# Adding x to the mixed terms on VectorE and GpSimd in the fourth layer, with its batches unrolled

## The reference

```
dx = shifted(x) - x
lerpx = x + dx * xw
lora(z, a, b, l) = l + tanh(z @ a.T) @ b.T
r = (x + dx * lora(lerpx, r_la, r_lb, r_ll)) @ rW.T      # and so k, v, g
w = exp(-exp(lora(x + dx * lora(lerpx, d_la, d_lb, d_ll), d_la, d_lb, d_ll)))
kv = k_i * v_j;  y_j = sum_i r_i * (st_ij + u_i * kv_ij);  st = w_i * st + kv     # per head of 8, per token
o = silu(g) * layernorm(y)
x = x + o @ oW.T + ternary_feed_forward(x)
```

## Time and profile before

| | |
|---|---|
| median of 3 runs | 2103.46 us (2102.39 to 2110.44) |
| the profiled execution: own time, span | 2104.47 us, 2102.6 us |
| TensorE busy, share of the span | 1796.5 us, 85% |
| VectorE | 1135.1 us, 54% |
| ScalarE | 925.1 us, 44% |
| GpSimd | 273.4 us, 13% |
| mean granted clock of TensorE | 0.927 |

### The profile page before, as it was taken

The page is one execution under the profiler, slowest core; times in us unless marked ns, Lnnn a source line. Parts: engine busy times, 40 slices in busy tenths (PEclk is TensorE's granted clock), DMA queues, the critical chain, the costliest instruction groups (busy, mean ns, idle before and its releaser), DMA issues. The chain is left out here.

```text
span 2102.6 us, 23302 instructions
## 1 busy us (share of the span) xinstructions
PE 1796.5 (85%) x7982; PEld 1032.2 (49%) x7982; DVE 1135.1 (54%) x1905; ACT 925.1 (44%) x1080; POOL 273.4 (13%) x159
## 2 busy tenths in 40 slices
PE   6699999983289996989899898989898996999996
PEld 3222222222144444666758585766667573444442
DVE  4445445437645556464453727264645535767765
ACT  4567677753022235353534344343535343444342
POOL 0000000002000004020200202020202003322321
PEclk8799999986599998999999999989999998999998
DMA  1222123310043310000000000000000010000000
GB/s 66 43 41 41 41 51 56 56 66 40 22 101 90 87 23 1 1 1 1 1 0 0 0 0 0 0 0 0 0 0 0 0 48 0 0 0 0 0 0 40
DMA packets 18927, 48.30 MB, mean 23 GB/s; under 512 B 640, under 2 KB 1408, under 8 KB 17856
## 3 DMA queue, kind: packets, MB, share of 16 engines
q1 hardware_dynamic: 18496, 47.53, 9.6%
q0 software_dynamic: 384, 0.13, 0.0%
HBM read 45.17 MB, written 2.36 MB: 23 GB/s over the span
## 5 line engine op out<-in xcount | busy, mean ns | idle before, releaser
L493 ACT ACTIVATE probs<-ps_ring 128x1024 f32<-128x1024 f32 x256 | 246.1, 1023 | 126.0 <-PE ps_ring L707 123.3
L1587 PEld LDWEIGHTS ps_o<-v,probs 128*128 128x128 f32 x2048 | 237.4, 192 | 4.9
L1587 PE MATMUL ps_o<-v,probs 128*128 128x129 f32 x2048 | 237.8, 275 | 0.0
L1404 DVE TENSOR_REDUCE max<-ps_o 128x1 f32<-128x512 f32 x256 | 167.9, 687 | 72.6 <-PE ps_o L1482 71.3
L1386 ACT ACTIVATE probs<-ps_wide 128x1024 f32<-128x1024 f32 x128 | 127.8, 1025 | 158.6 <-PE ps_wide L1492 158.5
L721 PE MATMUL ps_o<-probs,v 128*32 128x512 f32 x1024 | 141.5, 627 | 13.1 <-DVE o_sb L544 13.1
L1449 DVE RECIPROCAL rden<-ps_o 128x2 f32<-128x2 f32 x128 | 15.2, 160 | 244.9 <-PE ps_o L1587 244.9
L1350 ACT ACTIVATE probs<-ps_wide,pack 128x512 f32<-128x512 f32 x64 | 40.6, 685 | 212.2 <-PE ps_wide L1544 138.9
L1296 POOL TENSOR_TENSOR ql<-probs,qq 64x2048 fp32r<-64x2048 f32 x16 | 78.8, 4927 | 413.9 <-DVE qq L1422 411.6
L1544 PE MATMUL ps_wide<-probs,pack 128*128 128x512 f32 x256 | 121.6, 592 | 0.0
L1482 PE MATMUL ps_o<-kk,qq 128*128 128x512 f32 x256 | 117.9, 490 | 3.2
(11 more groups left out here) (349 smaller groups left out, 3385.0 us busy)
## 6 DMA issues: line engine op xcount, KB each, us to landing
cwb<-combine_by_expert SPq DMA_DIRECT2D x8, 2048.0 KB
score<-score_by_expert SPq DMA_DIRECT2D x8, 2048.0 KB, 13.7
pack<-pack_dram SPq DMA_DIRECT2D x1, 2560.0 KB, 13.8
pack<-pack_dram SPq DMA_DIRECT2D x1, 2443.0 KB, 9.5
x<-x_in SPq DMA_DIRECT2D x2, 1024.0 KB, 6.0
out<-x SPq DMA_DIRECT2D x1, 2048.0 KB, 6.3
pack<-pack_dram SPq DMA_DIRECT2D x1, 1547.0 KB, 8.1
pack<-pack_dram SPq DMA_DIRECT2D x1, 1288.5 KB, 16.5
```

The costliest lines, as they stand in the source:

```text
L493: nc.scalar.activation(probs[n % 3][:, 2 * half:2 * half + 2, :], ps, ACT.Exp, scale=float(HD0) ** -0.5).then_inc(read, 1)
L1404: nc.vector.reduce_max(top[:, u // NBLK, u % NBLK:u % NBLK + 1], ps_o[1][:, u % 2, :], AX_X).then_inc(max_read, 1)
L1587: last = nc.tensor.matmul(out, probs[:, (h + 1) % 2, m, n * P:(n + 1) * P], v[:, m, h, :], start=(m == 0), stop=(m == NBLK - 1))
```

## The change

`r`, `k`, `g` and `la_dd` get one product each, of `dmix` with `xn` already in it. The add for `d` is made by VectorE right behind its mix. The adds for `r`, `k` and `g` are made by GpSimd, behind `rs_4`, `rs_6` and `rs_7`; for these VectorE, behind each mix, drains and increments a semaphore (`mixed`) for which GpSimd waits. TensorE waits for the sums (`d_ready`, `sum_ready`) instead of for the mixes. The loop over the turns is a Python loop now, so its seven turns are written out in the program and their waits are against constants.

```diff
-            with eng.Fori(0, B - 1) as b:
+            for b in range(B - 1):
                 turn_program(Turn(b, b + 1))
...
         @block.gpsimd
+            def add_x(a, name):
+
+                pool.wait_ge(mixed, a * 3 + "rkg".index(name) + 1)
+                nc.gpsimd.tensor_tensor(dmix[name][:, :], dmix[name][:, :], xn[:, at(a)], ALU.add).then_inc(sum_ready, 1)
...
                         nc.gpsimd.tensor_tensor(rs[:, j % 4, :], r[:, :], st[:, j, :], ALU.mult).then_inc(rs_ready, 1)
+                        if a is not None and j in (4, 6, 7):
+                            add_x(a, {4: "r", 6: "k", 7: "g"}[j])
+                elif a is not None:
+                    for name in "rkg":
+                        add_x(a, name)
...
         @block.vector
                     nc.vector.scalar_tensor_tensor(to[:, :], src, w[f"ll_{name}"], dx[:, :],
                                                    ALU.add, ALU.mult).then_inc(read(f"lb_{name}"), 1)
+                    if name == "d":
+                        dve.drain()
+                        nc.vector.tensor_tensor(to[:, :], to[:, :], xn[:, at(a)], ALU.add).then_inc(d_ready, 1)
+                    elif name in "rkg":
+                        dve.drain()
+                        dve.sem_inc(mixed, 1)
...
         @block.tensor
-                    written("lb_d")
-                    product("la_dd", ("la_d", xn[:, at(a)]), ("la_d", dmix["d"][:, :]))
+                    pe.wait_ge(d_ready, a + 1)
+                    product("la_dd", ("la_d", dmix["d"][:, :]))
...
-                        written(f"lb_{n}")
-                        product(n, (f"{n}W", xn[:, at(a)]), (f"{n}W", dmix[n][:, :]))
+                        pe.wait_ge(sum_ready, a * 3 + "rkg".index(n) + 1)
+                        product(n, (f"{n}W", dmix[n][:, :]))
...
-                    written("lb_g")
-                    product("g", ("gW", xn[:, at(a)]), ("gW", dmix["g"][:, :]))
+                    pe.wait_ge(sum_ready, a * 3 + 3)
+                    product("g", ("gW", dmix["g"][:, :]))
```

More of the change, by code:

```diff
@@ L1671, in layer3_mix @@
         xv_ready = sem("xv_ready")
+        mixed, sum_ready, d_ready = sem("mixed3"), sem("sum_ready3"), sem("d_ready3")
         vw_high_ready, vw_ready = sem("vw_high_ready"), sem("vw_ready")
@@ L1943, in lora @@
                     product(name, (f"lb_{of}", th[tanh_of[3:]][:, :]))
-                def written(of):
-                    pe.wait_ge(ring_read[turn.bank(of)], turn.earlier(of) + 1)
                 def up(t):
```

## The result

| | before | after |
|---|---|---|
| median of 20 runs each | 2106.84 us (2102.17 to 2110.44) | 2112.68 us (2107.18 to 2119.73) |
| ratio, 95% interval | | 1.0027 (1.0017 to 1.0037) |
| the profiled execution: own time, span | 2104.47, 2102.6 us | 2107.18, 2105.3 us |

The change costs 0.27%, or 5.7 us (3.6 to 7.8 by the interval). That is less than the 0.5% from which the prediction counts a change, so no change, as forecast, and 2112.68 lies in the range of 2099 to 2115; but the forecast was +3.7 us, and its sum doesn't hold term by term.

A forecast was written before the change was run, and what follows sets the result against it. TensorE was taken as the bound (38.6 of 40.4 us per turn), VectorE close behind. Turns +1.7, first turn +2.3, entry -0.3 make +3.7 us: 2108.2 for the profiled execution, 2107 for the median; range 2099 to 2115.

The forecast's parts named there:

- GpSimd doesn't wait for a scan: Rival, steady turn: only scans wait for GpSimd; `yc` 0.6 us earlier than before, total about -4, 2100 us; chance 0.12.
- the full gain: Rival: scans and adds don't collide, the saving comes through whole, 19 us in seven turns, 2085 us; chance 0.06.
- the falling clock: Rival: TensorE idles more per turn, its clock falls, six turns take 1.3 us more each, +7.8, 2115 us; chance 0.12.
- the prediction's bound of 2111 us from a later hand-over: Two hand-overs to GpSimd in a turn cost 0.28 us more each, about 4 us in all, if release follows VectorE's end.
- the step list: The steady turn worked out operation by operation from `rs_4` to `yc`, with scans and GpSimd's operations waiting for each other.
- yc +0.33: Steady turn: both sides use up the 2.57 us saved, and `yc` comes at 28.69 instead of 28.36, 0.33 us later.
- unrolling −0.09: Each turn, at the add into `x`: a wait against a register goes, taking 0.09 us off; fetching longer code costs nothing.
- the first turn +2.3: First turn: GpSimd's adds delay its ternary work, which alternates with VectorE's; last ternary operation at 1777.0 instead of 1774.68.
- The entry to the loop −0.3: Entry to the turns: TensorE starts 0.1 instead of 0.39 us behind the last ternary operation, 0.3 us gained once.
- TensorE's 2.57 us: Each turn, ahead of `yc`: the three `xn` products removed from `la_dd`, `r` and `k` save 2.57 us.
- the 0.17 of the earlier trace: Another layer: a waiting GpSimd subtraction stood until about 0.17 us before the end of VectorE's cast.

The follow-up runs named there:

- The half adds: Changed kernel with each of GpSimd's three adds over 256 of the 512 tokens only: 2102.39 us, ratio 0.9980, turn 39.5 us.
- the memsets: Changed kernel with each of GpSimd's three adds replaced by a memset of a tile nobody reads: 2096.02 us, ratio 0.9957, turn 38.9 us.
- the kernel without adds: Changed kernel with GpSimd's three adds replaced by a semaphore increment, VectorE's new instructions kept: 2098.87 us, ratio 0.9963, turn 38.9 us.
- the kernel with the ternary work ahead: Changed kernel with GpSimd making its ternary weight before it waits for the first turn's mixes: 2110.59 us, ratio 1.0010, turn 41.1 us.
- `d` alone: Kernel before, loop kept, only `d` summed by VectorE; `r`, `k`, `g` keep two products each: 2098.64 us, ratio 0.9959, turn 39.6 us.

## Why the prediction held, and where its sum was off

**The number.** The forecast of 2107 was worked out from a median of 2103.46 for the kernel before, of three runs; twenty runs give 2106.84. Of the 5.5 us between the sum's 2107.2 and the measured 2112.68, 3.4 lie there and 2 in the change's own terms. That the sum is off by no more is partly luck, since two errors of opposite sign meet in it: the turns were forecast too low by 0.46 us each (3.2 in seven), and the first turn with the entry to the loop too high by 1.7.

**The mechanism.** Scans and GpSimd's operations on SBUF wait for each other, in both directions, seen in the turn itself: `scan_5`, `scan_6`, `scan_7` at 1.84, 2.09 and 2.16 us (forecast 1.7 to 2.4), the add of `r` at 2.18 (forecast near 2), the cast at 1.33 (over 1). `pick_7` waits 1.65 us for `rs_7` (forecast 2), the turn of 41.1 us lies just above the forecast 40.4 to 41, and the first full turn starts 0.2 us later and not 2, if the clock's part is left out (below). The rival "GpSimd doesn't wait for a scan" falls with the 2.18 us, the full gain with the 41.1 us of the turn, the falling clock with 1.00 in it. (That rival let TensorE's idle time in a turn grow from 2.4 to 5.5 us; by the stretches it grew from 1.8 to 4.8.) The hand-over to GpSimd came 0.21 us ahead of `scan_5`'s recorded end and not behind it, so the prediction's bound of 2111 us from a later hand-over lies near the measured time by chance. From `rs_4` to the end of `rs_7` the step list gives 11.12 us, and the rows 11.13. The half adds, the memsets and the kernel without adds show the cause independently of this list.

**Term "yc +0.33": too small by 0.50.** Counted from the start of the turn, `yc` came at 31.76 us instead of 30.93, so +0.83. The parts:
- mix `d` 0.10 later. I had taken from the written-out code only what it gives; it also takes: `rs` begins 0.15 us behind a scan instead of 0.08. The kernel with only the turns written out shows the same, 0.11.
- the add of `d` 0.84 us instead of 0.69, +0.15: it meets `rs_2`. With the loop kept it takes 0.76. I had compared the mixes and `kv` with `rs`, not this add.
- `rs_4` 0.07 later for the same reason as mix `d`, and 0.03 up to `scan_4`, 0.01 in the `rs` chain.
- from the end of `rs_7` to `y` 3.42 instead of 3.29, +0.13: the add of `g` ends 1.67 us behind `rs_7` instead of 1.59, and the cast that it holds 1.96 instead of 1.82.
- 0.01 from there to `yc`.

**Term "unrolling −0.09": right at its place, wrong for the whole.** From `yc` to the start of the next turn 9.34 us instead of 9.47, so −0.13. But the 0.10 us by which mix `d` is late belong to the unrolling too, and the kernel with nothing else changed has a turn of 40.4: in all it is nothing. The turn is +0.70 (+0.83 − 0.13, 41.1 against 40.4) and not +0.24. Six such intervals lie in the profile: 4.2 us.

**Term "the first turn +2.3": wrong.** The fourth layer's first stretch, up to the first add into `x` (so with the first full turn in it), takes 71.95 us, before 71.94. GpSimd and VectorE after:

```profile
1761.95 1.93 POOL L1695 TENSOR_SCALAR mag<-pack,bound 128x512 f32<-128x512 f32 x1
...
1763.34 0.69 DVE L1877 TENSOR_TENSOR xv_low<-xv,xv_high 128x512 fp32r<-128x512 f32 x1
...
1766.11 1.60 DVE L1698 TENSOR_TENSOR tern<-tern,mag 128x512 f32<-128x512 f32 x1
...
1770.80 1.52 DVE L1854 SCALAR_TENSOR_TENSOR ruk<-r,pack,k 128x512 f32<-128x512 f32 x1
```

and VectorE before:

```profile
1770.90 0.69 DVE L1880 SCALAR_TENSOR_TENSOR gate<-tg,ps_ring 128x512 f32<-128x512 f32 x1 [2.98 <-ACT tg L1789]
```

The two engines do take turns in their two-input ternary operations (1.60, 1.42 and 1.60 us on VectorE where 0.69 is needed). But I had let all of the work take turns, and the one-input operations hardly do: `xv_low` ran its 0.69 us beside `mag_1`. So from mix `d` to the last ternary operation it is 16.57 us instead of 15.91, +0.66 and not +2.3.

The collision itself isn't small: the kernel with the ternary work ahead shows it at 3.1 us. What stands against it is a gain that the prediction doesn't name: TensorE has four products less in the first turn too. `tg`, for which VectorE stood 2.98 us ahead of `gate`, is ready 12.10 us behind mix `d` before, and 9.45 after and 9.46 with the ternary work ahead. Without the collision that makes the stretch 2.4 us shorter than before (13.49 against 15.91), with it 0.66 longer.

`lerp`, no longer beside GpSimd's ternary work, takes 0.74 us instead of 1.19, which I hadn't counted. Another 1.0 us lies between `lerp` and mix `d`, and is TensorE's clock: its first six matmuls took 5.46 us in the execution profiled before, at a granted clock of 0.50, which is the lower level, and 4.46 after, at 0.63. This may well belong to the change: the three profiled kernels that keep the loop all have 5.46 there, the eight with the turns written out 4.2 to 4.5. Why isn't shown.

**The entry to the loop −0.3: right for TensorE, but it doesn't arrive.** TensorE starts 0.09 us behind the last ternary operation instead of 0.39. But GpSimd's `dx` now runs there and holds VectorE's `ruk` to 1.52 us instead of 0.75, and the first `kv` starts 2.19 us behind the last ternary operation instead of 2.07: +0.12. From that `kv` to the add into `x` the first full turn takes 39.92 us instead of 39.26. So the first stretch adds up: 0.66 − 0.45 − 1.0 + 0.12 + 0.66 is 0.

**The last turn.** It takes 38.05 us instead of 36.65, which I had at no change. TensorE, after, as it comes out of its longest wait, and the same place before:

```profile
2064.82 1.52 PE L1952 MATMUL ps_y<-rs,pack 128*128 128x512 f32 x2 [3.20 <-POOL rs L1739]
2066.14 3.19 PE L1968 MATMUL ps_f<-xn,pack 128*128 128x512 f32 x4
```

```profile
2063.24 1.10 PE L1935 MATMUL ps_y<-rs,pack 128*128 128x512 f32 x2 [3.04 <-POOL rs L1733]
2064.18 1.88 PE L1953 MATMUL ps_f<-xn,pack 128*128 128x512 f32 x4
```

A pair of matmuls takes 1.52 us behind 3.20 us of idleness, and 1.10 behind 3.04; the four matmuls that follow take 3.19 us after and 1.88 before. So this is the clock as well. It doesn't follow from the length of the wait: with only the turns written out the pair takes 2.04 behind 2.89. The last turn is short, 36.6 us, in the profiles of the kernel before and of the one with `d` and `r` on VectorE, and 37.5 to 38.6 in the nine others, which are all the written-out ones and, with the loop kept, the one with `d` alone. Each is a single execution, so whether writing the turns out makes the long one more frequent stays open.

**The sum.** By the two profiles the fourth layer is 5.7 us longer: 0 in the first stretch, 4.3 in six turns (0.72 each, by the mean), 1.4 in the last. (The spans differ by 2.7 only, since the three layers in front, which the change doesn't touch, took 3.0 us less in the execution profiled after.) The medians differ by as much, which is partly chance, since the first stretch and the last turn hold clock differences of single executions. Put right without these, the forecast is 7 × 0.7 in the turns and +0.33 in the first (0.66 − 0.45 + 0.12), +5.2 us, inside the interval of 3.6 to 7.8.

**Where TensorE's 2.57 us went.** From 40.4 they should have led to 37.8. Without GpSimd's adds the turn is 38.9: 1.1 us are lost. By the rows that is VectorE becoming the bound, with the add of `d`, three drains, and a scan that has lost the wait which kept it clear of `rs_4`; how the 1.1 us divide among these wasn't measured. GpSimd's adds take 2.2 more.

## What to carry to other kernels

An idle engine isn't a free one. Before work goes to GpSimd, look at what VectorE does at that time: if both read two SBUF operands, the moved work can lie on VectorE's path (here three adds of 1.27 us, which VectorE does in 0.69 each, cost 2.2 us a turn on a GpSimd that was idle for 29 of 40), and it pushes the next operation of each engine into the other's. When an engine that others wait for gets faster, count first how much waiting the next engine has left ahead of the point that binds; here it was 2.4 us in two places, and the sum of `d` alone fitted in without loss. And work that is taken away counts everywhere it stood: the first turn lost four products too. So do one part at a time: `d` alone gave 0.41%, all four together, with the turns written out, cost 0.27%.

## What the runs showed of the hardware

- Beside a one-input GpSimd operation the exclusion doesn't last for the whole of it: before, `lerp` (1750.17) began beside `mag_1` (1750.11, 1.59 us), took 1.19 us instead of 0.74 and ended 0.34 us ahead of it.
- GpSimd's memset and a VectorE scan don't disturb each other (1.14 and 1.28 us, side by side), while a memset does hold an f32 cast (0.73 instead of 0.43 us).
- The hand-over to the waiting engine comes before the recorded end of the other operation: the add of `r` had 1.27 us to run from 1913.24 on, and `scan_5` ends at 1913.45, so 0.21 us ahead. That is near the 0.17 of the earlier trace rows in the same direction.
- In written-out code with constant waits `rs` begins 0.15 us behind the scan's recorded end, in the loop 0.08. The last turn of the kernel before, which stands outside the loop, has 0.15 as well (`scan_1` 2062.35 and 1.82, `rs_1` 2064.32). The cause isn't shown.
- TensorE's granted clock was 1.00 in the steady turn of 41.1 us, in which it waited 1.65 us for `rs_7`; with all adds on VectorE, where it waited 2.5 us there, four of six turns had 0.96 and two 1.00.
